# The ratio of two expert gates: an exponential on ScalarE before, a power of e on GpSimd after

## The reference, cut to what matters

```python
logits = jnp.einsum('bsh,eh->bse', x, Wr)
probs = jax.nn.softmax(logits, axis=-1)
top_v, top_i = jax.lax.top_k(probs, K)
top_v = top_v / jnp.sum(top_v, axis=-1, keepdims=True)
...
    out = out + y * w_e[..., None]
```

## Time and profile before

| | us |
|---|---|
| median of 3 runs | 757.51 |
| lowest, highest | 754.78, 759.88 |
| span of the profiled execution | 767.7 |
| busy in it: PE, DVE, ACT, POOL | 663.8, 504.3, 400.6, 321.2 |
| groups 0 to 6 in it, from the first L1561 of body 0 (93.99) to that of group 7 (515.93) | 421.9 |

### The profile page before, as it was taken

One profiled execution on the slowest core, in us unless ns is written; L12 is line 12 of the kernel. 1 busy time (PEld: TensorE's weight loads), 2 busy tenths in 40 slices (PEclk: granted clock), 3 DMA queues, 4 the chain that ended last, 5 costly groups with the idle time before them and its releaser, 6 DMA issues.

```text
span 767.7 us, 20050 instructions
## 1 busy us (share of the span) xinstructions
PE 663.8 (86%) x6278; PEld 493.5 (64%) x6278; DVE 504.3 (66%) x1733; ACT 400.6 (52%) x855; POOL 321.2 (42%) x463
## 2 busy tenths in 40 slices
PE   9779898898998998998998989888888999999920
PEld 9664756755755764764774765674443999999920
DVE  4586568768679669668678777773624555555535
ACT  0212365484475375475465466544320677767716
POOL 6104362354364264265166157136014355444535
PEclk8579999999999999999999999999989999999965
DMA  8600000000000000000000000000032322222144
GB/s 294 214 1 14 2 29 17 1 25 14 4 25 14 4 21 14 7 21 11 11 18 14 11 0 32 11 0 29 1 111 86 78 72 72 71 68 73 53 173 173
DMA packets 26058, 36.23 MB, mean 47 GB/s; under 512 B 7302, under 2 KB 18311, under 8 KB 25736
## 3 DMA queue, kind: packets, MB, share of 16 engines
q1 hardware_dynamic: 20582, 22.72, 9.6%
q0 software_dynamic: 4576, 9.53, 3.6%
q10 hardware_dynamic: 850, 3.38, 1.3%
HBM read 23.99 MB, written 12.63 MB: 48 GB/s over the span
## 4 chain that ended last, share of the span: by engine, by line
PE 53%; DVE 15%; issue 12%; POOL 9%; ACT 6%; DMA 3%; SPq 1%; ACTq 1%; DVEq 1%; POOLq 0%
PE bank L1893 8%; PE bank L1903 8%; PE bank L1561 8%; PE bank L1735 4%; ACT mix L555 4%; POOL rstd L737 3%; PE bank L1597 3%; PE bank L1721 3%; PE bank L1701 3%; PE bank L1646 2%; PE bank L1654 2%; PE bank L1547 2%; POOL vare L734 2%; PE bank L1484 2%; POOL expert_in L779 1%
## 5 line engine op out<-in xcount | busy, mean ns | idle before, releaser
L779 POOL DMA_INDIRECT expert_in<-xb_rows,slot_u x72 | 73.2, 1016 | 103.5 <-PE bank L1711 49.0
L871 POOL DMA_INDIRECT expert_out<-xa,v_sb x71 | 68.3, 962 | 77.5 <-issue 47.3
L675 ACT ACTIVATE hT<-bank,qT 128x128 f32<-128x128 f32 x284 | 80.9, 368 | 36.6 <-issue 19.4
L734 POOL TENSOR_SCALAR vare<-mv 128x1 f32<-128x1 f32 (+1 forms) x108 | 23.8, 220 | 166.4 <-DVE mv L1064 166.1
L1186 DVE TENSOR_REDUCE negmax<-bank 128x4 f32<-128x512 f32 x128 | 79.4, 683 | 7.9 <-PE bank L1701 7.9
L555 ACT ACTIVATE mix<-bank 128x512 f32<-128x512 f32 x128 | 66.1, 605 | 24.9 <-PE bank L1721 24.9
L1903 PE MATMUL bank<-w_t,hT 128*128 x568 | 75.4, 276 | 1.1 <-ACT hT L675 1.1
L1893 PE MATMUL bank<-xnT,qT 128*128 128x128 f32 x568 | 75.1, 276 | 1.1 <-DVE qT L1400 1.1
L737 POOL TENSOR_TENSOR rstd<-vare,minus_half 128x1 f32<-128x1 f32 (+1 forms) x108 | 66.5, 616 | 9.6 <-POOL vare L734 1.2
L1903 PEld LDWEIGHTS bank<-w_t,hT 128*128 128x128 f32 x568 | 69.1, 192 | 1.8 <-issue 1.7
L1893 PEld LDWEIGHTS bank<-xnT,qT 128*128 128x128 f32 x568 | 69.0, 192 | 1.4 <-DVE qT L1400 1.4
(11 more groups left out here) (300 smaller groups left out, 1483.6 us busy)
## 6 DMA issues: line engine op xcount, KB each, us to landing
v_sb<-expert_in SPq DMA_DIRECT2D x71, 66.0 KB
w_t<-in_w_t ACTq DMA_DIRECT2D x1, 2064.0 KB, 7.3
x_all<-in_x SPq DMA_DIRECT2D x4, 512.0 KB, 7.9
xT_all<-in_xT SPq DMA_DIRECT2D x4, 512.0 KB, 8.6
ctxT<-in_ctxT SPq DMA_DIRECT2D x8, 256.0 KB
w_t<-in_w_t SPq DMA_DIRECT2D x1, 2048.0 KB, 8.7
x_all<-expert_out SPq DMA_DIRECT2D x4, 512.0 KB, 10.5
mix<-expert_out SPq DMA_DIRECT2D x3, 512.0 KB, 7.3
```

The source lines that it names most:

```text
L675: ins = nc.scalar.activation(hx[j % 2][:, c, :], bank[2 + j % 2][:, c * P:(c + 1) * P], ACT.Gelu, bias=w1c[j % 2][:, FF + c:FF + c + 1])
L779: nc.gpsimd.indirect_dma_start(xs[:, :], bass.IndirectOffsetOnAxis(ap=slot_u[:, t, k:k + 1], axis=0), xb_rows[k][:, t, :], None).then_inc( ...
L871: nc.gpsimd.indirect_dma_start(ys[:, :], bass.IndirectOffsetOnAxis(ap=tag[j % ROWS][:, HOME - P:HOME - P + 1].bitcast(U32), axis=0), ysb[j ...
```

## The change

ScalarE no longer computes the ratio. GpSimd does, as the elementwise power of a constant tile `euler` (128x4, filled once with e) to the power `below`, in the same kind of instruction as the norms' power. It stands behind the four third-norm scales and ahead of `group_sum(g + 1)`; in the last group, behind the LNB scales.

```diff
+        euler = sb("euler", [P, T])
...
                 nc.scalar.activation(xb_rows[1][:, :, 0:P], xb[:, :, :], ACT.Copy).then_inc(xb_copied, 1)
-                act.wait_ge(below_ready, g + 1)
-                nc.scalar.activation(ratio[:, :], below[:, :], ACT.Exp).then_inc(ratio_ready, 1)
                 if not last:
                     drain(g, "xh3T", xnT[:, :])
...
+            nc.gpsimd.memset(euler[:, :], math.e).then_inc(pool_const, 1)
...
-            pool.wait_ge(pool_const, 10)
+            pool.wait_ge(pool_const, 11)
...
+            def second_ratio(g):
+                pool.wait_ge(below_ready, g + 1)
+                pool.sem_inc(pool_held, 1)
+                nc.gpsimd.tensor_tensor(ratio[:, :], euler[:, :], below[:, :], ALU.pow).then_inc(ratio_ready, 1)
...
                     ln_scale(LN3, g + 1, 3)
+                second_ratio(g)
+                if not last:
                     group_sum(g + 1)
```

More of the change, by code:

```diff
@@ L1 @@
 from contextlib import ExitStack
+import math
 import numpy as np
```

## The result

The changed kernel takes 769.25 us (median of 4 runs, 767.37 to 771.53) against 758.03 us of the kernel before (4 runs): a ratio of 1.0164, with a 95% interval of 1.0129 to 1.0200. It is 11.2 us slower. The forecast was 757.8 us, no change, with 761.5 as the upper end.

What follows compares the result with a forecast made beforehand. Boundaries between loop bodies end last on the route DVE, `slot_u`, POOL, `xa`, not on PE. Six boundaries at 0.14 us less 0.5 in the last group made +0.3 on the median 757.51, so 757.8 us; range 752.5 to 761.5.

Steps and rivals of the forecast that it cites:

- ScalarE's part: On ACT, 15 table loads (19.2 us) and eight ratios go; almost none of it was counted on the path.
- the rival that had the loads on the path: All 15 table loads on the path would give 19.2 us, so 738 us; chance 4%.
- Steps 1 to 4: At the boundary: power 0.20 us behind `below`, lasting 1.05; `group_sum` after it, lateness covered; last third norm freed, gaining 0.43.
- Step 4: DVE's last third norm is no longer held by `group_sum`: 0.43 us gained for `xh3T`, `high` and `ff1`.
- Step 5: DVE's `wsum` begins 0.06 us into the moved `group_sum` and is held, ending at 214.09 instead of 213.36.
- Step 6: Behind `wsum` on DVE, `slot_u` and POOL's whole route come 0.14 us later; six boundaries cost 0.84 us.
- The term of 6 × 0.14 us: Cost of the later `slot_u` and POOL route over six loop boundaries: 0.84 us.
- The last group: In the last group `ff1` ends 0.43 us earlier and `ff2` starts at about 520.1, a gain of 0.5 us.
- The signs: Changed profile: 15 loads fewer, `xn` without 0.75, `wsum` held, `low` not waiting for `high`, `xbk` 0.1 us later, power 1.05.
- The slow power: The power at the 128x8 form's cost, 0.61 us more in each of six boundaries: 761.5 us; chance 15%.
- "Not held": `wsum` is not held by the sum, so `low` starts 0.3 us earlier: 755.2 us, or 754.4 with nothing held; chance 25%.
- The page against the change: The skill says POOL contends with some DVE instructions; the prediction applied it to `wsum`, held, with the sum as made.

Runs made afterwards that it cites:

- run 2: The changed kernel with the group sum ahead of the power, where it stood before; 757.99 us, ratio 1.0005 to the kernel before.
- Run 1: The changed kernel with six more small products on TensorE in each loop body, ahead of the rank products; 758.69 us, ratio 1.0004 to the kernel before.
- Run 6: The changed kernel with `chosen` made by a one-input reduction in place of a two-input addition; 757.35 us, ratio 0.9983 to the kernel before.
- runs 5 to 8: The changed kernel with sum behind `chosen` (758.02 us); `chosen` by one-input reduction (757.35); sum in four parts ahead of the power (754.62); that plus earlier decay product (750.44).
- run 5: The changed kernel with the group sum behind GpSimd's wait for `chosen`; 758.02 us, ratio 0.9982 to the kernel before.
- run 4: The changed kernel with the group sum cut into four one-tile sums, the fourth behind the power; 755.12 us, ratio 0.9963 to the kernel before.
- run 3: The kernel before, exponential kept, with a power that nobody reads ahead of the group sum in seven loop bodies; 771.73 us, ratio 1.0191.

## Why the prediction was wrong

- **ScalarE's part** was right. The loads went, 15 of them, and run 2 shows that they are worth nothing here; with it the rival that had the loads on the path is gone.
- **Steps 1 to 4** were right but for `ff1`. The power began 0.18 us behind `below` (forecast 0.20) and took 1.02 us (forecast 1.05); the sum began 0.04 us before the end of the power; `xn` fell from 0.75 to 0.33 us, and `high` came 0.42 us earlier against `below`. Step 4 had `ff1` 0.43 us earlier too; it started 3.40 us behind `below` (215.97 − 212.57) and not 2.69, 0.71 later.
- **Step 5** failed in which instruction is held. It had `wsum` begin 0.06 us behind the sum, after a free `chosen`. By the same working `chosen` would begin at 213.10 − 0.43 = 212.67, only 0.06 us ahead of the sum at 212.73, and the prediction passed over it without a word; on the chip it began 0.01 us behind, as the sum came 0.06 us earlier than forecast (213.90 against 212.73 + 1.23 = 213.96). A case that hangs on 0.06 us should have been priced on both sides. That DVE's queue would be held to the sum's end came right by luck, through another instruction than the one forecast, and so did the times behind it: `low` at 215.71 (forecast 214.50 + 1.23 = 215.73), `slot_u` 4.68 us behind `below` against 4.56, 0.12 us later (forecast 0.14). `low` no longer waits for `high`, as forecast.
- **Step 6** is where the time was lost: "Behind `wsum` DVE queues the reciprocals, the product L1321, `low`, the ranks and `slot_u`, and POOL waits for that." That followed only one engine from the held instruction. TensorE was left out: its rank products wait for `chosen`, and `ff1` is queued behind them, though `ff1` needs nothing of it. Run 1 shows that even this wait would have been nearly free: 758.69 us, 0.8 above the kernel before, where the forecast added 0.3. What the wait set off was not: 1.62 us more in `ff1` (5.29 − 3.67) at the lower clock, and no term of the sum and no rival had a place for that. The term of 6 × 0.14 us was 6 × 1.74. Run 6, in which `chosen` is free and `wsum` is held as forecast, takes 757.35 us; so what the prediction had for its own case, no change that could be measured, was right.
- **The last group**, −0.5 us in the sum, came out at +2.1 by the same cause. In runs 5 to 8, where `chosen` is free or nearly so, `ff2` starts 6.62 to 6.64 us behind `below` there, 0.6 less than before: the term was right for that case.
- **The signs** could not have shown the error. All came true (15 loads, `xn` without 0.75, `wsum` begun only at the sum's end, `low` no longer waiting for `high`, `xbk` 0.12 us later against the start of `xn`, the power at 1.02 us), and none looked at TensorE.
- **The rivals.** The slow power had the right sign and the wrong cause; the power was as fast as forecast. "Not held" was wrong, as both runs 5 and 6 show a hold on an instruction of 4 numbers a partition.
- **The page against the change** pointed at a part of the error. The Trainium skill (GPSIMD Engine Reference, section 8) names DVE instructions with two SBUF inputs among those that contend with POOL. `chosen` has two, and held, while its version with one input ran free; the runs agree with the page. It was weighed for `wsum` alone, and not for each instruction near the sum.

## What to carry to other kernels

Before a large GpSimd operation is moved, list every VectorE instruction that can begin within its span, and for each one of the kinds that were held here (an addition or a product with two SBUF inputs, or a float32 TENSOR_SCALAR from SBUF to SBUF as `xn` and `wsum` are) ask who waits for it: a hold that VectorE's own queue absorbs can stop TensorE, where unrelated products are queued behind the wait. Look at the idle time that TensorE gets, and at what stands behind it; six small products in that gap were worth 10.6 us here. Work taken off an engine that did not end last gave nothing by itself here (run 2), and the instruction put in its place moves whatever is queued behind it.

## What the runs showed of the hardware

A hold lasted for the whole of what was left of POOL's instruction, whatever the size of VectorE's: 1.29 us for `chosen`, begun 0.01 us into the sum, 1.10 us for a product of 4 numbers a partition (run 5), 0.47 us where POOL's own took 0.46 (run 4). Not every instruction was held: inside a sum the reduction took 0.22 us (run 6), the reciprocal 0.15 (run 5), and in the kernel before each of the four index searches 0.16 (L1300, from 211.50 on). The Trainium skill (SBUF — State Buffer, SBUF: two separate sides) describes an exclusive lock that whoever starts first keeps for the whole instruction; these rows agree.

Behind a pause of 1.42 us and eight short products TensorE's granted clock was 0.50 to 0.53 over the first 3.1 to 3.2 us of `ff1` in every boundary of the changed kernel, while behind the same pause in the first boundary of run 3 it was 1.00, and `ff1` took 3.67 us. The power of e cost what the power to −1/2 of that shape did, 1.02 against 1.05 us.
